# First attention of a gated cross-attention kernel on one Trainium2 core: 154 keys split as 128 and 26 in place of 77 and 77

## The chip, the core and the metric

The kernel is one program on one NeuronCore of a Trainium2 chip. The metric is device time in microseconds (us), the median of several executions. The engines are TensorE (PE in the rows, its weight loads PEld), VectorE (DVE), ScalarE (ACT), GpSimd (POOL) and SyncE (SP). PSUM has eight banks of 128 partitions by 512 fp32 values.

## The reference

Two blocks in series, each a gated cross-attention and a gated feed-forward part, with a residual stream x of 2 x 1024 tokens of 256 values. The change is in the first of the four parts:

```
x = x + tanh(g_xattn[0]) * xattn0(layernorm(x), ctx, ctx, W, b)     # the part that changes
x = x + tanh(g_ffn[0])   * ffn0(layernorm(x), Wg, Wu, Wd)            # 8 experts, all of them for every token
x = x + tanh(g_xattn[1]) * xattn1(layernorm(x), ctx, mask, ...)      # 8 heads of 64
x = x + tanh(g_ffn[1])   * ffn1(layernorm(x), wg, We, be)            # one of 8 experts by argmax, with a capacity

def xattn0(query, key, value, W, b):        # one head of 256; ctx is 2 x 154 x 256
    q, k, v = query @ W.T + b, key @ W.T + b, value @ W.T + b
    return softmax(q @ k.T / 16) @ v
```

## The kernel before

All engines run programs written out by hand, tied by semaphores: an engine takes its own instructions in the order written, and the order below is the whole schedule. Nothing is planned or reordered by a tool.

The 2048 tokens are 16 tiles of 128, and 4 chunks (`u` = 0 to 3) of 4 tiles; chunks 0 and 1 belong to batch 0, 2 and 3 to batch 1. In the first attention keys and values are the same tensor k0 = ctx @ W.T + b, held transposed as `k0T` (feature on the partition, 308 keys along the row). TensorE's preparation ends with `v_transposes` (L1307 to L1316): eight transposes of 128 x 77 pieces of `k0T` into banks 1 and 2, which ScalarE copies to `V0` (L970), keys on 77 partitions, two halves for each batch.

For each chunk TensorE then does, in the loop after L1379:

- `a_scores` (L1333): scores of four tiles, two per bank, in banks 4 and 5 or 6 and 7 (`UNIT_PS`). From chunk 2 on each of its two halves waits for `a_res`, the residual add of that half two chunks earlier (L1338).
- `a_p_transposes` (L1349): eight transposes of the exponentials `PA`, 77 keys of a tile at a time, into banks 1 and 2. ScalarE copies them to `PTA` (L936).
- the transposes of a later chunk's normed rows (L1296), `x1_transposes` or `x2_transposes`.
- `a_attend` (L1356): for each tile two matmuls over 77 keys each, `PTA` against `V0`, added up in half a bank. After tiles 0 and 1 it signals the first half on `a_out_ps`, after tiles 2 and 3 the second (L1362).

An fp32 matmul is two records in the trace, an fp32 transpose one. VectorE takes row maxima (`a_maxes`, L1947, L1952), and adds the attention into `x_res` (`a_add`, L1968), two tiles for each half, with a signal on `a_res` after each half. Its list in order after chunk 0's maxima is: norm of chunk 2, maxima 1, statistics 3, `a_add(0)`, maxima 2, statistics of chunk 0's result, small mask work, `a_add(1)`, statistics, maxima 3, norm, `a_add(2)`, then sums and roundings of the operands of the first feed-forward part (`xop_raw` L1978, `xop_lo` L490), `a_add(3)` among them. GpSimd splits expert weights between its small steps (L619 to L661); each round starts at a norm of VectorE (`pool.wait_ge(a_ln1, 2)`, then `a_ln2, 1`).

Bank 5 (`R0_PS`) holds the bias row's product until VectorE has read it (L1929, L1931), and after that chunk 0's scores of tiles 2 and 3.

## Time and profile before

| | us |
|---|---|
| median of 3 executions | 1226.97 (1226.01 to 1227.29) |
| span of the profiled execution | 1225.2 |
| that execution's own time | not listed apart from the span; the median is 1.8 above the span |
| TensorE busy | 1199.5 (98% of the span) |
| VectorE busy | 1051.4 (86%) |
| ScalarE busy | 739.6 (60%) |
| GpSimd busy | 886.6 (72%) |
| first attention, in the span | about 18 to 54 |
| first feed-forward part | 54 to about 998 |

The span runs from the first to the last instruction of the profiled execution. A busy share says nothing by itself: the feed-forward part is nine tenths of the span, and the change lies ahead of it, in a stretch where several engines wait for one another.

### The profile page before, as it was taken

The numbers are of one execution on the slowest core, as the hardware profiler recorded it, in microseconds if no ns is written. First come the engines' busy times: TensorE is split into PE (matmuls) and PEld (weight loads), VectorE is DVE, ScalarE is ACT, GpSimd is POOL, SyncE is SP. The second block draws the span as 40 slices with busy tenths as digits, with TensorE's granted clock in tenths as the row PEclk, the third lists the DMA queues.
The fourth block names the chain that finished last, engine by engine and source line by source line (L and its number), as shares of the span: only waits on it lengthen the run. The fifth ranks groups of instructions, "written<-read, shape, count | busy, mean of one in ns | idle before, by whom it ended". The sixth has DMA issues, their size and how long they took to land.

```text
span 1225.2 us, 18428 instructions
## 1 busy us (share of the span) xinstructions
PE 1199.5 (98%) x6143; PEld 987.8 (81%) x6143; DVE 1051.4 (86%) x1754; ACT 739.6 (60%) x1531; POOL 886.6 (72%) x848
## 2 busy tenths in 40 slices
...
DMA packets 42365, 48.27 MB, mean 39 GB/s; under 512 B 4239, under 2 KB 40143, under 8 KB 42015
## 3 DMA queue, kind: packets, MB, share of 16 engines
...
## 4 chain that ended last, share of the span: by engine, by line
PE 89%; DVE 5%; ACT 3%; issue 1%; ACTq 1%; POOL 0%; POOLq 0%; DVEq 0%
PE bank L1400 25%; PE bank L1402 25%; PE bank L1401 25%; ACT PC L1124 3%; PE bank L1643 2%; PE bank L1652 1%; PE bank L1822 1%; DVE nmC L2204 1%; PE bank L1805 1%; PE bank L1345 1%; PE bank L1755 1%; DVE stats L1879 1%; PE bank L1577 1%; PE bank L1627 1%; PE bank L1578 1%
## 5 line engine op out<-in xcount | busy, mean ns | idle before, releaser
L1400 PE MATMUL bank<-xop_hi,w_hi 128*128 128x512 f32 x896 | 349.2, 390 | 1.9 <-DVE half_g L2028 0.9
L1402 PE MATMUL bank<-xop_hi,w_lo 128*128 128x512 f32 x896 | 348.6, 389 | 0.0
L1401 PE MATMUL bank<-xop_lo,w_hi 128*128 128x512 f32 x896 | 348.6, 389 | 0.0
L2063 DVE TENSOR_TENSOR hid_lo<-hid,hid_hi 128x512 fp32r<-128x512 f32 x228 | 232.5, 1044 | 6.0 <-ACT hid_hi L1042 6.0
L1400 PEld LDWEIGHTS bank<-xop_hi,w_hi 128*128 128x128 f32 x896 | 168.2, 188 | 37.9 <-DVE half_g L2028 1.3
L1402 PEld LDWEIGHTS bank<-xop_hi,w_lo 128*128 128x128 f32 x896 | 168.2, 188 | 35.0
L1401 PEld LDWEIGHTS bank<-xop_lo,w_hi 128*128 128x128 f32 x896 | 168.2, 188 | 34.7
L1042 ACT CAST hid_hi<-hid 128x512 fp32r<-128x512 f32 x228 | 140.8, 622 | 63.6 <-PE bank L1402 38.3
L1026 ACT ACTIVATE s<-bank 128x512 f32<-128x512 f32 x128 | 78.2, 611 | 95.2 <-PE bank L1402 95.2
L1400 PE MATMUL bank<-hid_hi,wd_hi 128*128 128x512 f32 x344 | 134.2, 390 | 0.7 <-DVE hid_lo L2063 0.6
L1401 PE MATMUL bank<-hid_lo,wd_hi 128*128 128x512 f32 x344 | 133.9, 389 | 0.0
L1402 PE MATMUL bank<-hid_hi,wd_lo 128*128 128x512 f32 x344 | 133.9, 389 | 0.0
L1002 ACT COPY bank<-bank 128x512 f32<-128x512 f32 x128 | 73.2, 573 | 67.9 <-PE bank L1402 67.9
L2087 DVE TENSOR_TENSOR acc<-bank,acc 128x512 f32<-128x512 f32 x136 | 93.0, 684 | 20.4 <-PE bank L1402 20.3
L1032 ACT ACTIVATE half_g<-half_g 128x512 f32<-128x512 f32 x128 | 81.1, 634 | 46.8 <-DVE half_g L2036 25.5
L2055 DVE TENSOR_TENSOR hid<-half_u,half_g 128x512 f32<-128x512 f32 x128 | 107.2, 875 | 0.0
L702 POOL TENSOR_TENSOR t_loT<-t_rawT,t_hiT 128x512 fp32r<-128x512 f32 x56 | 84.2, 1526 | 16.4 <-ACT t_hiT L1049 16.4
L2046 DVE TENSOR_TENSOR hid<-bank,s 128x512 f32<-128x512 f32 x128 | 86.6, 676 | 1.2 <-PE bank L1402 1.2
L648 POOL TENSOR_TENSOR w_lo<-w_raw,w_hi 128x1024 fp32r<-128x1024 f32 x32 | 77.5, 2421 | 2.9 <-ACT w_hi L1063 2.9
L796 POOL TENSOR_TENSOR PC<-PC,rdenC 128x616 f32<-128x616 f32 x32 | 38.9, 1216 | 53.5 <-DVE rdenC L2212 53.4
L1400 PEld LDWEIGHTS bank<-hid_hi,wd_hi 128*128 128x128 f32 x344 | 64.6, 188 | 15.3 <-DVE hid_lo L2063 1.0
L1402 PEld LDWEIGHTS bank<-hid_hi,wd_lo 128*128 128x128 f32 x344 | 64.6, 188 | 13.5
(288 smaller groups left out, 2608.3 us busy)
## 6 DMA issues: line engine op xcount, KB each, us to landing
...
```

Of the source, the lines that this page charges most:

```text
L648: nc.gpsimd.tensor_tensor(out=lo[:, :, W_S1:W_S4 + 1], in0=s[:, :, W_S1:W_S4 + 1], in1=hi[:, :, W_S1:W_S4 + 1].bitcast(F32), op=ALU.subtra ...
L702: nc.gpsimd.tensor_tensor(out=t_lo[i][:], in0=t_raw[i][:], in1=t_hi[i][:].bitcast(F32), op=ALU.subtract).then_inc(t_ready, 1)
L1026: nc.scalar.activation(out[:], ps[:], ACT.Silu).then_inc(silu_ready[h], 1)
L1032: nc.scalar.activation(half["g"][:], half["g"][:], ACT.Silu).then_inc(silu_ready[h], 1)
L1042: nc.scalar.copy(hid_hi[n % 2][h][:], hid[h][:]).then_inc(hi_ready[h], 1)
L1400: mm(ps, w, a, start=start, stop=False, skip_group_check=True)
L1401: mm(ps, w, a_low, start=False, stop=False, skip_group_check=True)
L1402: return mm(ps, w_low, a, start=False, stop=True, skip_group_check=True)
L2046: nc.vector.tensor_tensor(out=hid[h][:], in0=ps[:], in1=s[:], op=ALU.mult).then_inc(hid_ready[h], 1)
L2055: nc.vector.tensor_tensor(out=hid[h][:], in0=half["u"][:], in1=half["g"][:], op=ALU.mult).then_inc(hid_ready[h], 1)
L2063: nc.vector.tensor_tensor(out=hid_lo[n % 2][h][:], in0=hid[h][:], in1=hid_hi[n % 2][h][:].bitcast(F32), op=ALU.subtract).then_inc(lo_ready ...
L2087: nc.vector.tensor_tensor(out=to, in0=ps, in1=to, op=ALU.add).then_inc(acc_added, 1)
```

## The change

The 154 keys of a batch are taken as 128 and 26. The two tiles of an output bank pair use different ends: tiles 0 and 1 of a chunk (`i` = 0) take keys 0 to 127 and then 128 to 153, tiles 2 and 3 (`i` = 1) take keys 26 to 153 and then 0 to 25. The rests stand on partitions 0 to 25 for `i` = 0 and 32 to 57 for `i` = 1, so that the matmuls over 26 keys of two tiles in different banks use different row groups of TensorE. `PA` gets slots of 160 columns, the last six of them set to zero once by GpSimd, so that the rests of two tiles can be transposed together as 64 columns. `V0` holds, for each batch, both choices of 128 keys, and a new `V0R` the rests; eight matmuls by the identity, 26 keys each, make them in bank 5. ScalarE's wait and signal counts move by one, and TensorE's wait for the values (`V0_OUT`) now stands ahead of the second half of chunk 0's scores, since that half uses bank 5.

```diff
     B, S, D = x.shape
     KEYS = ctx.shape[1]
     KH = KEYS // 2
+    REST, RW = KEYS - P, 32
+    SLOT = P + RW
+    FIRST_KEY, REST_KEY = (0, REST), (P, 0)
+    V0R_PS = 5
     NE0, _, F = Wg.shape
     INNER = Wq.shape[1]
     HD = 64
...
     C_VALUES = 2 + HB // 2
     PREP_DVE = 4
-    NORMED0, A0_OUT, V0_OUT, NORMED20 = 5, 6, 8, 9
+    NORMED0, A0_OUT, V0_OUT, NORMED20 = 5, 6, 9, 10
     R_MID, R_LOW = 32, 64
     R_ROWS = R_LOW + 1
-    PREP_PE = 10
+    PREP_PE = 11
     FIRST_SEVEN = 3
...
-        V0 = keep.take("V0", [KH, 2 * B, D], F32)
+        V0 = keep.take("V0", [P, B, 2, D], F32)
+        V0R = keep.take("V0R", [2 * RW, B, D], F32)
         stats, mv, ve, rstd, shift = [], [], [], [], []
...
-        PA = sa.take("PA", [P, 2 * CT, KEYS], F32)
-        PTA = sa.take("PTA", [KH, 2, 2, CH], F32)
+        PA = sa.take("PA", [P, 2 * CT * SLOT], F32)
+        PTA = sa.take("PTA", [P, 2, CH], F32)
+        PTR = sa.take("PTR", [2 * RW, 2, 2 * P], F32)
         nmA, nmsA, denA, rdenA, coefA = (sa.take(n, [P, NT], F32) for n in ("nmA", "nmsA", "denA", "rdenA", "coefA"))
         mask8 = sa.take("mask8", [P, AK], U8, size=1)
...
+            steps.did(nc.gpsimd.memset(PA[:].rearrange("p (n k) -> p n k", k=SLOT)[:, :, KEYS:SLOT], 0.0))
...
                     n = u * CT + j
-                    ins = nc.scalar.activation(PA[:, u % 2 * CT + j, :], bank[UNIT_PS[u % 2][j // 2]][:, j % 2 * 256:j % 2 * 256 + KEYS], ACT.Exp,
+                    at = (u % 2 * CT + j % 2 * 2 + j // 2) * SLOT
+                    ins = nc.scalar.activation(PA[:, at:at + KEYS], bank[UNIT_PS[u % 2][j // 2]][:, j % 2 * 256:j % 2 * 256 + KEYS], ACT.Exp,
                                                bias=nmsA[:, n:n + 1], scale=D ** -0.5, accum_out=denA[:, n:n + 1])
                 ins.then_inc(a_probs, 1)
 
             def a_pT_out(u):
-                for k in range(2):
-                    act.wait_ge(a_pT_ps, 2 * u + k + 1)
-                    nc.scalar.copy(PTA[:, u % 2, k, :], bank[PT_PS[k]][0:KH, :]).then_inc(a_pT, 1)
+                act.wait_ge(a_pT_ps, 2 * u + 1)
+                nc.scalar.copy(PTA[:, u % 2, :], bank[PT_PS[0]][:]).then_inc(a_pT, 1)
+                act.wait_ge(a_pT_ps, 2 * u + 2)
+                nc.scalar.copy(PTR[:, u % 2, :], bank[PT_PS[1]][0:2 * RW, 0:2 * P]).then_inc(a_pT, 1)
 
             def x_raw_out(u):
...
             a_xnT_out(0)
+            for b in range(B):
+                act.wait_ge(prep_pe, 9 + b)
+                nc.scalar.copy(V0[:, b, :, :].rearrange("p k d -> p (k d)"), bank[V0_PS[b]][:]).then_inc(prep_act, 1)
+            act.wait_ge(prep_pe, 11)
             for i in range(2):
-                act.wait_ge(prep_pe, 9 + i)
-                nc.scalar.copy(V0[:, 2 * i:2 * i + 2, :].rearrange("p k d -> p (k d)"), bank[V0_PS[i]][0:KH, :]).then_inc(prep_act, 1)
+                row = slice(i * RW, i * RW + REST)
+                ins = nc.scalar.copy(V0R[row, :, :].rearrange("p b d -> p (b d)"), bank[V0R_PS][row, :])
+            ins.then_inc(prep_act, 1)
             a_xnT_out(1)
...
                 pe.wait_ge(prep_dve, 4)
+                for b in range(B):
+                    for i in range(2):
+                        key = b * KEYS + FIRST_KEY[i]
+                        for m in range(KB):
+                            ins = tr(bank[V0_PS[b]][:, i * D + m * P:i * D + (m + 1) * P], k0T[:, m, key:key + P], ident[:])
+                    ins.then_inc(prep_pe, 1)
                 for i in range(2):
-                    for r in range(2):
+                    for b in range(B):
+                        key = b * KEYS + REST_KEY[i]
                         for m in range(KB):
-                            ins = tr(bank[V0_PS[i]][0:KH, r * D + m * P:r * D + (m + 1) * P],
-                                     k0T[:, m, (2 * i + r) * KH:(2 * i + r + 1) * KH], ident[:])
-                    ins.then_inc(prep_pe, 1)
+                            ins = mm(bank[V0R_PS][i * RW:i * RW + REST, b * D + m * P:b * D + (m + 1) * P],
+                                     k0T[:, m, key:key + REST], ident[:], start=True, stop=True, skip_group_check=True)
+                ins.then_inc(prep_pe, 1)
 
...
                 pe.wait_ge(a_probs, u + 1)
-                for k in range(2):
-                    for j in range(CT):
-                        ins = tr(bank[PT_PS[k]][0:KH, j * P:(j + 1) * P], PA[:, u % 2 * CT + j, k * KH:(k + 1) * KH], ident[:])
-                    ins.then_inc(a_pT_ps, 1)
+                first = u % 2 * CT * SLOT
+                for j in range(CT):
+                    i, a = j // 2, j % 2
+                    at = first + (2 * a + i) * SLOT + FIRST_KEY[i]
+                    ins = tr(bank[PT_PS[0]][:, j * P:(j + 1) * P], PA[:, at:at + P], ident[:])
+                ins.then_inc(a_pT_ps, 1)
+                for a in range(2):
+                    at = first + 2 * a * SLOT + P
+                    ins = tr(bank[PT_PS[1]][0:2 * RW, a * P:(a + 1) * P], PA[:, at:at + 2 * RW], ident[:])
+                ins.then_inc(a_pT_ps, 1)
 
             def a_attend(u):
                 pe.wait_ge(a_pT, 2 * u + 2)
-                for j in range(CT):
-                    for k in range(2):
-                        ins = mm(bank[UNIT_PS[u % 2][j // 2]][:, j % 2 * D:(j % 2 + 1) * D], PTA[:, u % 2, k, j * P:(j + 1) * P],
-                                 V0[:, u // CB * 2 + k, :], start=k == 0, stop=k == 1)
-                    if j % 2:
-                        ins.then_inc(a_out_ps, 1)
+                b = u // CB
+
+                def out_of(i, a):
+                    return bank[UNIT_PS[u % 2][i]][:, a * D:(a + 1) * D]
+
+                for a in range(2):
+                    for i in range(2):
+                        j = 2 * i + a
+                        mm(out_of(i, a), PTA[:, u % 2, j * P:(j + 1) * P], V0[:, b, i, :], start=True, stop=False)
+                    for i in range(2):
+                        row = slice(i * RW, i * RW + REST)
+                        ins = mm(out_of(i, a), PTR[row, u % 2, a * P:(a + 1) * P], V0R[row, b, :], start=False, stop=True)
+                        if a == 1:
+                            ins.then_inc(a_out_ps, 1)
 
             def x2_transposes(u):
                 pe.wait_ge(a_xnT, KB * NC)
...
             pe.wait_ge(prep_dve, 4)
             a_scores(0, [0])
             x1_transposes(1)
+            pe.wait_ge(prep_act, V0_OUT)
             a_scores(0, [1])
             for u in range(NC):
                 if u + 1 < NC:
                     a_scores(u + 1)
-                if u == 0:
-                    pe.wait_ge(prep_act, V0_OUT)
                 a_p_transposes(u)
                 if u + 2 < NC:
                     x1_transposes(u + 2)

```

On TensorE, in the preparation and chunk 0, the rows were these (`k0T` keys transposed, `ones_r` the bias part of the scores, `A` their weights, `xnA` normed rows):

```order
L1314 MATMUL bank<-ident,k0T 77x128 [waits prep_dve,prep_act]
L1314 MATMUL bank<-ident,k0T 77x128 x7
L1340 MATMUL bank<-r_56,ones_r 128x2x154 [waits a_xnT,prep_dve]
L1345 MATMUL bank<-A_55,xnT 128x154 x4
L1296 MATMUL bank<-ident,xnA 128x128 [waits a_ln1,a_xnT]
L1296 MATMUL bank<-ident,xnA 128x128 x7
L1340 MATMUL bank<-r_56,ones_r 128x2x154 [waits a_xnT]
```

Now they are:

```order
L1329 MATMUL bank<-ident,k0T 128x128 [waits prep_dve,prep_act]
L1329 MATMUL bank<-ident,k0T 128x128 x7
L1335 MATMUL bank<-ident,k0T 26x128 x8
L1361 MATMUL bank<-r_56,ones_r 128x2x154 [waits a_xnT,prep_dve]
L1366 MATMUL bank<-A_55,xnT 128x154 x4
L1310 MATMUL bank<-ident,xnA 128x128 [waits a_ln1,a_xnT]
L1310 MATMUL bank<-ident,xnA 128x128 x7
L1361 MATMUL bank<-r_56,ones_r 128x2x154 [waits a_xnT,prep_act]
```

Eight small matmuls came in ahead of the first scores, and the second half of the scores waits for ScalarE as well. Also on TensorE, the transposes of the exponentials and the values' matmuls of one chunk, before:

```order
L1353 MATMUL bank<-ident,PA 77x128 [waits a_probs]
L1353 MATMUL bank<-ident,PA 77x128 x7
L1296 MATMUL bank<-ident,xnA 128x128 [waits a_ln1,a_xnT]
L1296 MATMUL bank<-ident,xnA 128x128 x7
L1360 MATMUL bank<-V_57,PTA 128x256 [waits a_pT]
L1360 MATMUL bank<-V_57,PTA 128x256 x7
```

and now:

```order
L1376 MATMUL bank<-ident,PA 128x128 [waits a_probs]
L1376 MATMUL bank<-ident,PA 128x128 x3
L1380 MATMUL bank<-ident,PA 64x128 x2
L1310 MATMUL bank<-ident,xnA 128x128 [waits a_ln1,a_xnT]
L1310 MATMUL bank<-ident,xnA 128x128 x7
L1393 MATMUL bank<-V_57,PTA 128x256 [waits a_pT]
L1393 MATMUL bank<-V_57,PTA 128x256
L1396 MATMUL bank<-V0R,PTR 128x256 x2
L1393 MATMUL bank<-V_57,PTA 128x256 x2
L1396 MATMUL bank<-V0R,PTR 128x256 x2
```

Eight transposes became six; eight matmuls over 77 keys became four over 128 and four over 26, with tiles 0 and 2 ahead of tiles 1 and 3. On ScalarE the copies of the values, before and now:

```order
L923 COPY xnT<-bank 128x512 [waits a_xnT_ps] x2
L970 COPY V_57<-bank 77x512 [waits prep_pe] x2
L923 COPY xnT<-bank 128x512 [waits a_xnT_ps] x2
```

```order
L930 COPY xnT<-bank 128x512 [waits a_xnT_ps] x2
L979 COPY V_57<-bank 128x512 [waits prep_pe] x2
L983 COPY V0R<-bank 26x512 [waits prep_pe]
L983 COPY V0R<-bank 26x512
L930 COPY xnT<-bank 128x512 [waits a_xnT_ps] x2
```

Two copies of the rests came in between.

## Rows read from the trace of the kernel before

**Rows 1.** The page: busy time of TensorE, share of the span, instructions.
```profile
PE 1199.5 (98%) x6143; PEld 987.8 (81%) x6143; DVE 1051.4 (86%) x1754; ACT 739.6 (60%) x1531; POOL 886.6 (72%) x848
```
**Rows 2.** Busy time in two stretches, with the granted clock (of 1) after PEclk.
```profile
40.62:49.88 9.26, 9.26 (x65) 8.69 (x66) 7.45 (x25) 6.09 (x18) 5.75 (x10) 1.00 0.27 87
66.39:1225.20 1158.81, 1140.75 (x5823) 941.41 (x5823) 1001.00 (x1608) 699.92 (x1436) 850.71 (x772) 1.00 0.11 37
```
**Rows 3.** Timeline of TensorE, preparation's end: start, us, engine, line, operation, count, [idle before].
```profile
19.01 1.07 PE L1314 MATMUL bank<-ident,k0T 128*77 128x128 f32 x8 [0.34 <-DVE A L1938]
...
21.10 1.04 PE L1296 MATMUL bank<-ident,xnA 128*128 128x128 f32 x8
...
22.11 1.21 PE L1345 MATMUL bank<-A,xnT 128*128 128x154 f32 x8
```
**Rows 4.** Timeline of ScalarE, the same stretch.
```profile
19.68 1.07 ACT L970 COPY V<-bank 77x512 f32<-77x512 f32 x2 [0.33 <-PE bank L1314]
```
**Rows 5.** Timeline of TensorE, chunks 0 and 2, values and what follows.
```profile
27.60 3.72 PE L1360 MATMUL bank<-V,PTA 77*128 77x256 f32 x16
31.39 0.29 PE L1340 MATMUL bank<-r,ones_r 65*128 65x308 bf16 x1
...
40.62 0.29 PE L1340 MATMUL bank<-r,ones_r 65*128 65x308 bf16 x1 [1.39 <-DVE x_res L1968]
...
44.74 3.72 PE L1360 MATMUL bank<-V,PTA 77*128 77x256 f32 x16
```
**Rows 6.** Timeline of TensorE, second attention: 64 rows on two groups, then 128.
```profile
1059.77 0.70 PE L1604 MATMUL bank<-k1T,qT 64*128 64x154 f32 x8
1060.40 0.33 PE L1511 MATMUL bank<-ident,acc 128*128 128x128 f32 x1
```
**Rows 7.** Timeline of TensorE, second attention: 128 columns of output, then 64.
```profile
1066.59 0.55 PE L1627 MATMUL bank<-ident,PC 128*128 128x128 f32 x3
1067.08 2.24 PE L1643 MATMUL bank<-PTC,V 128*64 128x128 f32 x34
```
**Rows 8.** Timeline of VectorE, chunk 0's add to chunk 2's maxima.
```profile
33.95 0.48 DVE L1947 TENSOR_REDUCE nmA<-bank 128x2 f32<-128x308 f32 x1 [0.70 <-PE bank L1345]
34.47 1.60 DVE L1952 TENSOR_SCALAR nmsA<-nmA 128x4 f32<-128x4 f32 x1
...
39.60 1.66 DVE L1968 SCALAR_TENSOR_TENSOR x_res<-bank,coefA,x_res 128x256 f32<-128x256 f32 x4
```
**Rows 9.** Timeline of VectorE, chunk 2's add and after it.
```profile
44.11 0.17 DVE L1952 TENSOR_SCALAR nmsA<-nmA 128x4 f32<-128x4 f32 x1
...
48.56 0.88 DVE L1968 SCALAR_TENSOR_TENSOR x_res<-bank,coefA,x_res 128x256 f32<-128x256 f32 x2 [0.85 <-PE bank L1360]
49.88 0.69 DVE L1978 TENSOR_TENSOR xop_raw<-bank,xop_raw 128x512 f32<-128x512 f32 x1 [0.44 <-PE bank L1296]
50.60 0.82 DVE L490 TENSOR_TENSOR xop_lo<-xop_raw,xop_hi 128x512 fp32r<-128x512 f32 x1
```
**Rows 10.** Timeline of GpSimd, three of its steps.
```profile
25.41 0.72 POOL L619 TENSOR_TENSOR w_raw<-raw_gu 128x256 f32<-128x256 f32 x1 [2.10 <-DVE xnA L1892]
...
33.68 2.37 POOL L648 TENSOR_TENSOR w_lo<-w_raw,w_hi 128x1024 fp32r<-128x1024 f32 x1
...
49.84 1.04 POOL L632 CAST w_hi<-w_raw 128x1024 fp32r<-128x1024 f32 x1
```
**Rows 11.** The chain that ended last, where TensorE's unbroken stretch begins.
```profile
66.39 0.50 PE bank L1400
```
**Rows 12.** Lengths of one record or weight load, ns: least/median/most, first and last start.
```profile
L1604 PE MATMUL bank<-k1T,qT x256: 288/291/291, 1020.0 to 1163.8; 64*128 64x154 f32 x128
...
L1643 PE MATMUL bank<-PTC,V x544: 270/273/472, 1028.2 to 1178.5; 128*64 128x128 f32 x171, 80*64 80x128 f32 x11
...
L1360 PEld LDWEIGHTS bank<-V,PTA x64: 186/190/190, 27.6 to 53.2; 77*128 77x128 f32 x64
L1360 PE MATMUL bank<-V,PTA x64: 379/379/483, 27.6 to 53.4; 77*128 77x256 f32 x64
```

## The prediction

> **What bounds the kernel now.** I read the busy shares first: TensorE is busy for 98% of the span [rows 1]. That alone would say that less work on TensorE is less time, so I read by stage. From 66.39 to the end TensorE works for 1140.75 of 1158.81 us [rows 2], and the chain of waits that ended last passes to TensorE at 66.39 [rows 11]. All that the change touches lies before. So the question is by how much the moment at 66.39 moves; what is behind it moves along.
>
> Ahead of it the chain alternates. From 19.01 TensorE carries it through the transposes of the keys and the first scores [rows 3]. From chunk 2's maxima (33.95) to the end of chunk 1's adds VectorE does [rows 8], and TensorE waits 1.39 us for it until 40.62 [rows 5]. From 40.62 to 49.88 TensorE is busy for 9.26 of 9.26 us [rows 2] at the full granted clock (1.00, its 2.4 GHz level), and VectorE waits for it twice (0.85 and 0.44 us) [rows 9]. Then VectorE carries it again.
>
> There is a second thing to see in VectorE's rows. A setting of four numbers per partition (L1952) takes 0.17 us at 44.11 [rows 9] but 1.60 at 34.47, ending at 36.07 [rows 8]; GpSimd's L648 ran from 33.68 to 36.05 [rows 10]. At 50.60 an L490 takes 0.82 and ends at 51.42 [rows 9]; GpSimd's L632 ends at 50.88 [rows 10]. I read both as VectorE being held until GpSimd's instruction ends. GpSimd's round starts when VectorE's norm is done (25.41) [rows 10], so it moves with the chain at its start.
>
> **The change, part by part.**
>
> *Values, in the preparation.* Eight transposes stay eight, at the same pace: eight of 77 columns take 1.07, eight of 128 take 1.04 [rows 3]. A record costs (1.04 - 0.27)/7 = 0.11, 0.27 being the last one's own length [rows 12]. Added are eight matmuls of 26 keys, 16 records of 128 columns, for which the trace has no row. The nearest is L1643, whose outputs also alternate between two column groups: 34 records in 2.24 us, (2.24 - 0.27)/33 = 0.06 each [rows 7], so two run side by side. Here one column group has the first four matmuls, the other the last four. Side by side they cost 8 x 0.11 = 0.88, one after the other 16 x 0.11 = 1.76.
>
> *Changes of tile shape.* From 64 rows back to 128, the last pair starts at 59.77 + 0.70 - 0.29 = 60.18 and the next instruction at 60.40: 0.22, where the pace is (0.70 - 0.29)/3 = 0.13 [rows 6, 12]. From 128 columns to 64, the last starts at 66.59 + 0.55 - 0.27 = 66.87 and the next at 67.08: 0.21 for 0.11 [rows 7]. So a change costs 0.09 to 0.10; I take 0.09. The values pay two: 0.88 + 0.18 = **+1.06**, all of it on the path, since the scores stand behind them in TensorE's list. The other end is 1.76 + 0.18 = 1.94. I take the lower, because L1643 ran side by side although each of its matmuls is two records as well.
>
> The Trainium skill (TensorE: Matmul & The Clock Gate, section Part 3: Packing small matmuls) says against this that matmuls keep strict program order, with no reordering. By that rule the second column group would start only with the end of the first, and this term would be near 1.8.
>
> *The new wait and the copies.* ScalarE copies two rests more, 1.07 for two copies of 512 columns [rows 4]. They can start near 19.01 + 0.88 + 1.06 + 0.2 = 21.2 and end at 22.3. TensorE reaches the wait at 21.10 + 0.88 + 1.06 = 23.04 [rows 3]: nothing, with 0.7 to spare. ScalarE's next copy, queued behind, waits for transposes that are later by 1.06 as well. Were the rests serial, copies and wait would both be later by the same. GpSimd's added memset of 48 columns is covered by the warm-up matmuls. Nothing.
>
> *Transposes of the exponentials.* Eight become six, with two changes if 64 columns are a shape of their own: 6 x 0.11 + 0.18 = 0.84 against 0.88, -0.04 for each chunk; -0.22 without the changes, +0.18 if 64 columns need two records each. ScalarE copies 64 x 256 in place of 77 x 512 and isn't later.
>
> *The values' matmuls.* A record of 256 columns costs (3.72 - 0.38)/15 = 0.22 [rows 5, 12]; sixteen were 3.56. Now four full matmuls are 8 records, the two pairs of rests 4 paces if they run side by side as L1604's two row groups do (eight records in 0.70) [rows 6], and four changes 0.36: 12 x 0.22 + 0.36 = 3.03. That is -0.53 for each chunk. With nothing side by side it is +0.36.
>
> *The late half.* The first half used to be signalled after half of the records. Now tiles 0 and 1 are done only when nearly all is. I follow it chunk by chunk.
>
> Chunk 0. Its values start at 27.60 + 1.06 - 0.04 = 28.62 and end 3.72 - 0.62 = 3.10 later, at 31.72 (one change comes after the end). VectorE starts 0.1 later (48.56 behind 44.74 + 3.72), adds a half in 0.88 [rows 5, 9], and TensorE follows 0.13 after: chunk 2's scores start at 32.83 in place of 31.39 [rows 5], +1.44. VectorE's L1952 could then end near 34.47 + 1.44 + 0.17 = 36.1. But GpSimd holds it to 36.05 + 1.06 = 37.11 anyway. Behind L1952 the shift is +1.06 again: the late half has cost nothing, with 1.0 to spare.
>
> Chunk 1. Its values end near 40.0, VectorE wants them at 39.60 + 1.06 = 40.66 [rows 8]. Nothing, gain included.
>
> Chunk 2. Start 44.74 + 1.06 - 0.04 = 45.76, end 48.86, adds from 48.96, and four of them take 1.58 to the next instruction (1.66 less the overlap) [rows 8]: the first operand sum starts at 50.54 in place of 49.88, +0.66. Here 0.4 of the gain would show. But the L490 behind it meets GpSimd's L632, which now ends at 50.88 + 1.06 = 51.94, later than the 51.26 at which L490 starts. It ends 0.54 behind it as before [rows 9, 10]: +1.06.
>
> Chunk 3's values end about when they did, and the feed-forward part behind them waits for VectorE. Nothing.
>
> **The sum** is +1.06 at 66.39, a span of 1225.2 + 1.1 = 1226.3. What lies around the span (1.8 to the median of the runs) is taken as unchanged: 1226.97 + 1.1 = **1228.0**.
>
> **The rivals.** About 0.2% (2.5 us) is what a measurement of this kernel can tell from no change.
>
> *Not held.* If VectorE's long instructions aren't tied to GpSimd's end, chunk 0's L1952 ends at 36.1 and the shift falls to about 0. Chunk 2's values then end near 47.8, VectorE's adds near 49.5: -0.3, **1226.6**. Against it stand two ends that agree to 0.02 us [rows 8, 10]; for it, that phases of two engines are hard to foresee. 0.15.
>
> *In order.* If tiles are served in program order, the rests in the preparation overlap in one record only (+1.83) and each pair of rests takes three paces (+0.44 for each chunk). Chunk 0 is still covered by the hold; the end is +1.83, **1228.8**. Against it stands L1604 [rows 6]; for it, that four matmuls in a row on one group are more than any row shows. 0.22.
>
> *Dear changes, slower.* TensorE changes shape six times in each chunk and twice before. The 0.09 is from shapes of 64. If with 26 rows the array finishes a record (0.38) and then loads weights (0.19) with nothing overlapped [rows 12], a change costs 0.57 - 0.22 = 0.35. Then the preparation costs 1.58, each chunk's transposes +0.48 and its values about +0.51. Chunk 0's scores are late by over 3.4, past the cover of the hold, and the shift behind L1952 becomes about 2.1; chunk 2 brings it to +2.9, **1229.9**, slower. It decides from about 0.3 for each change. 0.13. The Trainium skill (TensorEngine Tiling (Array Packing), section Key Properties) says that changing the tiling mode drains the TensorE, and gives no figure; by it every one of these changes pays, and this rival is a matter of how much.
>
> Something that no row shows, either way: 0.08.
>
> **How the numbers follow.** My forecast has 0.42, in order 0.22, not held 0.15, dear changes 0.13, the unknown 0.08. The range of 8 in 10 reaches from not held less the scatter of the runs (1226.6 - 0.8) to a little over dear changes: 1225.8 to 1230.2. Slower by over 0.2% are dear changes and half of the unknown, 0.17; faster has no mechanism that I can price, 0.05 for the unknown and a lucky phase; within 0.2% 0.78. The predicted time is 1228.0.
>
> **What would show it.** In the profile after: eight matmuls L1335 in about 1.1 us (1.9 if in order); no wait ahead of the second scores; 16 records of `a_attend` in 3.1 in place of 3.72 (3.5 in order, 4.1 with nothing side by side); chunk 2's scores about 1.4 later, with L1952 ending when L648 does; TensorE's unbroken stretch from about 67.45. I am wrong if the feed-forward part changes its pace, if a change of shape takes over 0.2, or if L1952 is short while the shift behind it stays.

## The result, and the profile after

The changed kernel takes 1230.24 us, the median of five runs (1227.36 to 1232.03), against 1226.97 for five of the kernel before (1224.33 to 1227.33); the ratio is 1.0029, with a 95% interval of 1.0018 to 1.0040. I had forecast 1228.0 and a range up to 1230.2. So the change is slower by over 0.2%, the case to which I had given 0.17. Two further comparisons of the same kernel gave 1.0018 (1.0009 to 1.0027) and 1.0027 (1.0018 to 1.0036), with medians of 1229.62 and 1229.98. So 1230.24 lies just above the range, the two repeats just inside it; all three are well above 1228.0.

The profiled execution is the fastest of the five: 1227.36 us, with a span of 1225.6. Its span is within 0.4 us of that of the profile of before, although the medians are 3.3 apart. That is the first thing to explain. First the page of the changed kernel (answers to [rows 1]) and its stretches (to [rows 2]); the page rows give busy time, share of the span and instructions.

```profile
PE 1197.9 (98%) x6151; PEld 982.2 (80%) x6151; DVE 1049.6 (86%) x1754; ACT 739.8 (60%) x1533; POOL 886.2 (72%) x849
```
```profile
40.32:49.34 9.02, 9.02 (x63) 7.39 (x64) 7.28 (x24) 5.76 (x18) 5.56 (x9) 1.00 0.27 89
66.07:1225.60 1159.53, 1140.82 (x5823) 941.10 (x5823) 999.70 (x1608) 699.63 (x1436) 850.35 (x772) 1.00 0.11 37
```

The preparation and chunk 0's values on TensorE (timeline: start, us, engine, line, operation, count, [idle before]); these answer to [rows 3, 5].

```profile
15.90 1.04 PE L1310 MATMUL bank<-ident,xnA 128*128 128x128 f32 x8
17.17 1.06 PE L1329 MATMUL bank<-ident,k0T 128*128 128x128 f32 x8 [0.24 <-DVE A L1972]
18.17 1.52 PE L1335 MATMUL bank<-ident,k0T 128*26 128x128 f32 x16
19.61 0.30 PE L1361 MATMUL bank<-r,ones_r 65*128 65x308 bf16 x1
...
25.43 0.66 PE L1376 MATMUL bank<-ident,PA 128*128 128x128 f32 x4
25.92 0.38 PE L1380 MATMUL bank<-ident,PA 128*64 128x128 f32 x2
26.14 1.04 PE L1310 MATMUL bank<-ident,xnA 128*128 128x128 f32 x8
27.02 1.13 PE L1393 MATMUL bank<-V,PTA 128*128 128x256 f32 x4
28.08 0.70 PE L1396 MATMUL bank<-V0R,PTR 26*128 26x256 f32 x4
28.71 1.13 PE L1393 MATMUL bank<-V,PTA 128*128 128x256 f32 x4
29.77 0.70 PE L1396 MATMUL bank<-V0R,PTR 26*128 26x256 f32 x4
31.60 0.29 PE L1361 MATMUL bank<-r,ones_r 65*128 65x308 bf16 x1 [1.12 <-DVE x_res L2002]
...
66.07 0.50 PE L1434 MATMUL bank<-xop_hi,w_hi 128*128 128x512 f32 x1 [0.23 <-DVE half_u L2062]
```

The eight rest matmuls (L1335) take 1.52 us, neither the 1.1 of the forecast nor the 1.9 of the rival in order. Chunk 0's values take 29.77 + 0.70 - 27.02 = 3.45 in place of 3.72; I had written 3.1. Next, the holds on VectorE (to [rows 8 to 10]): VectorE, then GpSimd.

```profile
34.67 1.09 DVE L1986 TENSOR_SCALAR nmsA<-nmA 128x4 f32<-128x4 f32 x1
...
50.06 1.06 DVE L496 TENSOR_TENSOR xop_lo<-xop_raw,xop_hi 128x512 fp32r<-128x512 f32 x1
```
```profile
33.37 2.37 POOL L655 TENSOR_TENSOR w_lo<-w_raw,w_hi 128x1024 fp32r<-128x1024 f32 x1
...
49.54 1.04 POOL L639 CAST w_hi<-w_raw 128x1024 fp32r<-128x1024 f32 x1
```

L1986 ends at 35.76, GpSimd's L655 at 35.74. L496 ends at 51.12, 0.54 behind the end of GpSimd's L639 at 50.58, as it did before. Both holds are there as forecast. The other traces bear the first one out: in 19 of the 20 traces of this case the setting for chunk 2 takes 0.6 to 1.6 us and ends 0.02 to 0.03 behind GpSimd's instruction. In the twentieth (e1) GpSimd is done first, and the same setting takes 0.17. VectorE and GpSimd in e1:

```profile
38.23 0.17 DVE L1986 TENSOR_SCALAR nmsA<-nmA 128x4 f32<-128x4 f32 x1
```
```profile
35.27 2.35 POOL L655 TENSOR_TENSOR w_lo<-w_raw,w_hi 128x1024 fp32r<-128x1024 f32 x1
```

Not every instruction of GpSimd holds it, though: chunk 3's setting takes 0.17 (43.81 to 43.98) while GpSimd's L602, a power of 4 elements per partition, runs from 43.09 to 44.10. The Trainium skill (SBUF — State Buffer, section SBUF: two separate sides) says that GpSimd and those instructions of VectorE that are in a two-port mode or have two inputs in SBUF share a pair of ports, held for the whole instruction by whichever starts first. The ends beside L655 and L639 agree; no run here shows the ports, and L602 is a case in which nothing waited.

**One clock for all traces.** The start of the attention differs from execution to execution, since before it, between about 9 and 16 us, TensorE's granted clock is at 0.50 for 0, 3.4 or 6.8 us. So I measure from the start of chunk 0's row transposes (L1310, before L1296) to five starts on TensorE behind it. The last is the feed-forward matmul that waits for `half_u`, where TensorE's unbroken stretch begins (66.39 before [rows 11], 66.07 after). Each number is a difference of two starts in the timeline of TensorE; "low" is where the granted clock reads 0.50 between 16 us and that point.

| kernel | first scores | chunk 0 values | chunk 2 scores | chunk 3 scores | unbroken stretch | low at |
|---|---|---|---|---|---|---|
| before, as shown | 2.28 | 9.96 | 13.75 | 22.98 | 48.75 | none |
| before again (e15) | 1.85 | 9.54 | 13.32 | 22.55 | 48.32 | none |
| before again (e18) | 2.11 | 9.78 | 13.57 | 22.78 | 50.20 | 41.3 |
| after, as shown | 3.71 | 11.12 | 15.70 | 24.42 | 50.17 | none |
| change again (e1) | 3.69 | 11.09 | 15.66 | 25.80 | 51.55 | 33.8 |
| change again (e12) | 3.39 | 10.79 | 15.36 | 24.09 | 51.15 | 42.8 |
| change again (e16) | 3.39 | 10.80 | 15.37 | 24.10 | 49.87 | none |
| change again (e17) | 3.39 | 10.80 | 15.37 | 24.11 | 51.18 | 43.1 |

The rows behind the first and the last column for e15, then for e16: start of the row transposes, first scores, unbroken stretch.

```profile
18.92 1.04 PE L1296 MATMUL bank<-ident,xnA 128*128 128x128 f32 x8
20.77 0.29 PE L1340 MATMUL bank<-r,ones_r 65*128 65x308 bf16 x1
...
67.24 0.50 PE L1400 MATMUL bank<-xop_hi,w_hi 128*128 128x512 f32 x1 [0.24 <-DVE half_u L2028]
```
```profile
19.22 1.04 PE L1310 MATMUL bank<-ident,xnA 128*128 128x128 f32 x8
22.61 0.30 PE L1361 MATMUL bank<-r,ones_r 65*128 65x308 bf16 x1
...
69.09 0.50 PE L1434 MATMUL bank<-xop_hi,w_hi 128*128 128x512 f32 x1 [0.23 <-DVE half_u L2062]
```

The two traces first shown each have a small wait ahead of the key transposes (0.34 and 0.24) that e15, e12, e16 and e17 don't have. Without a low stretch the change moves the unbroken stretch by 49.87 - 48.32 = +1.55 (or 50.17 - 48.75 = +1.42). With one it comes 1.3 to 1.4 later still, and 1.6 in the kernel before (e18, measured from its first scores). Behind it the change costs nothing by itself: in the nine traces of this case without a low stretch in the second attention, of both kinds of kernel, the rest of the span is 1157.8 to 1158.2. In the eleven with one, starting between 1070 and 1119 us, it is 1158.8 (before, as shown) to 1159.8 (e12). So there is a second place where the clock falls, at a price of 0.8 to 1.8. Four of the five traces of the change have it (all but e17), one of the three of the kernel before. Over all kernels tried it is 8 of 15 with the split of 128 and 26, and 3 of 5 with 77 and 77, so nothing says that the change brings it.

The profile after looks good because its clock was full from the start (chunk 0's row transposes begin at 15.90, before at 17.64), and because it has no low stretch in the first attention: -1.74 to the row transposes, +1.42 to the unbroken stretch and +0.7 behind it make the 0.4. For the same reason the unbroken stretch begins at 66.07 and not at the 67.45 of the forecast, although the chain ahead of it is longer.

### The profile page after: what moved, and what is told of

Its sections match the earlier page's. It is cut to its first block, busy times and chain, and to the rows that moved or that the text cites. A ratio compares the mean times of both kernels' runs of the same rounds, so it can differ in the third digit from the quotient of the medians.

```text
span 1225.6 us, 18447 instructions
## 1 busy us (share of the span) xinstructions
PE 1197.9 (98%) x6151; PEld 982.2 (80%) x6151; DVE 1049.6 (86%) x1754; ACT 739.8 (60%) x1533; POOL 886.2 (72%) x849
## 4 chain that ended last, share of the span: by engine, by line
PE 89%; DVE 5%; ACT 4%; issue 1%; ACTq 1%; POOL 0%; POOLq 0%; DVEq 0%
PE bank L1434 25%; PE bank L1435 25%; PE bank L1436 25%; ACT PC L1138 3%; PE bank L1686 2%; PE bank L1677 1%; PE bank L1856 1%; DVE nmC L2238 1%; PE bank L1839 1%; DVE stats L1913 1%; PE bank L1366 1%; PE bank L1789 1%; PE bank L1611 1%; PE bank L1612 1%; PE bank L1616 1%
## 5 line engine op out<-in xcount | busy, mean ns | idle before, releaser
L655 POOL TENSOR_TENSOR w_lo<-w_raw,w_hi 128x1024 fp32r<-128x1024 f32 x32 | 77.4, 2420 | 2.9 <-ACT w_hi L1077 2.9
```

The costliest lines, as they stand in the source:

```text
L655: nc.gpsimd.tensor_tensor(out=lo[:, :, W_S1:W_S4 + 1], in0=s[:, :, W_S1:W_S4 + 1], in1=hi[:, :, W_S1:W_S4 + 1].bitcast(F32), op=ALU.subtra ...
```

## The experiments

Two theories are named in them. CLOCK: part of the loss is a granted clock that falls in the first attention. DIRECT: all of it is the work and waits of the change. PREPARATION, CHUNKS, SHAPE and PLACE are explained where they come. A *fall* is a low stretch that begins in the first attention behind a wait of TensorE.

**e1, the change again.**

> The changed kernel as it is, once more, for the clock and the span of each execution. In the five executions so far the mean granted clock was 0.998 in the one at 1227.36 and 0.994 to 0.996 in those at 1230.1 to 1232.0. Theory CLOCK: most of the 3.3 us is TensorE at its lower level in more stretches than before; then time falls with the granted clock along one line (about 1.2 us for each 0.001), an execution at 0.998 is near 1227.4, and a trace at 0.996 or less has stretches of granted clock 0.5 that the kernel before doesn't have, between 8 and 60 us or in the second attention. Theory DIRECT: instructions on the path (the values' rests at 1.5 us, the late half) make it; then the before and changed kernels differ by 3 us at the same granted clock, and the trace of an execution at 1230 shows the first feed-forward part starting 3 us later with no stretch at 0.5 between.

1229.62 us (1227.49 to 1231.37), ratio 1.0018. Its trace has the low stretch at 33.8 (table); this is what the stretches before and in it look like (columns as in [rows 2]).

```profile
30.30:33.80 3.50, 2.38 (x15) 1.31 (x12) 2.93 (x7) 1.37 (x7) 3.36 (x6) 0.99 0.01 2
33.80:37.10 3.30, 3.30 (x15) 3.19 (x15) 0.81 (x2) 1.71 (x4) 3.30 (x3) 0.50 0.00 0
```

TensorE was busy for 2.38 of 3.50 us, with its wait of 1.12 in them, and then ran chunk 2's scores at the 1.2 GHz level. My forecast had a granted clock of 1.00 for this stage from one trace, and asked no further. CLOCK was expected here to be most of the 3.3 us. That has not held: at an equal granted clock 1.9 us are left (under e16 to e18).

**e2, filled once.** Five wide matmuls of ones into a free bank behind chunk 0's values.

```diff
                 a_attend(u)
+                if u == 0:
+                    keep_busy(5, PT_PS[0])
```

> The change, with five warm-up matmuls (bf16, 128 x 512, 0.22 each, 1.1 in all) behind chunk 0's values, into bank 1, where TensorE waits 1.12 us for the late half. Theory CLOCK, if this wait is what lets the clock fall: the executions lose their low stretches, median near 1227.5 (-2.7). If the clock falls elsewhere: no change, 1230.2. Theory DIRECT: 1230.2 to 1230.5, since the fill lies in a wait.

1228.55 us, ratio 1.0015 (1.0006 to 1.0024); no low stretch in the attention; 50.06 to the unbroken stretch. That is 1.1 us under e1 in the median, but the intervals overlap, and CLOCK had expected 1227.5. By itself it settles nothing.

**e3, the first half early.** Tile by tile, its rest right behind its first matmul.

```diff
-                for a in range(2):
-                    for i in range(2):
+                for i in range(2):
+                    for a in range(2):
...
+                    ins.then_inc(a_out_ps, 1)
```

> The change, with the values' matmuls tile by tile (128 keys, then 26), tiles 0 and 1 first, so that the first half is signalled after half of the work again, and no two rests stand side by side. Each chunk's values take 16 records and 8 changes of shape, 16 x 0.22 + 8 x 0.08 = 4.2 in place of 3.0. Theory DIRECT (late half costs): chunk 2's scores start right behind the values (0.1) and the kernel is at or below the change (1229 to 1230). If the pairing is worth what it takes off TensorE: slower by up to 1.2 for chunk 2, 1231.4. Theory CLOCK: TensorE is busier between 26 and 40, so fewer low stretches: 1228 to 1229.

1230.65 us (1229.23 to 1231.86), ratio 1.0025 (1.0014 to 1.0035), and 51.56 to the unbroken stretch with no low clock: 1.7 later than e16. The chunks had been expected to become dearer, but CLOCK, which had 1228 to 1229 here, missed. The rows of its values:

```profile
29.93 0.70 PE L1393 MATMUL bank<-V,PTA 128*128 128x256 f32 x2
30.55 0.69 PE L1395 MATMUL bank<-V0R,PTR 26*128 26x256 f32 x2
31.18 0.70 PE L1393 MATMUL bank<-V,PTA 128*128 128x256 f32 x2
31.81 0.69 PE L1395 MATMUL bank<-V0R,PTR 26*128 26x256 f32 x2
```

Two records take 0.63 from start to start where the pace is 2 x 0.215 = 0.43 (0.22 in [rows 5, 12]). So each change of shape costs 0.20. In the profile after, 28.71 - 27.02 = 1.69 holds six paces (1.29) and two changes: 0.20 each again. I had 0.09. I had looked only at the interval across the change (0.31 here, 0.22 and 0.21 in [rows 6, 7]); the record behind it is late too (0.32). Splitting the pairs up to have the first half early is a loss.

**e4, alternating column groups.** The rest matmuls of the preparation in another order.

```diff
-                for i in range(2):
-                    for b in range(B):
-                        for m in range(KB):
+                for b in range(B):
+                    for m in range(KB):
+                        for i in range(2):
```

> The change, with the eight matmuls of the rests in the preparation in alternating order of their two column groups. They took 1.52 us in the group's order (0.08 for each record). If side by side works best when neighbours differ: 16 records in 1.1 to 1.2 us, and everything behind earlier by 0.35. If the order doesn't matter (the array looks ahead): 1.5 again. Time: -0.35 or 0 against the change at the same granted clock; theory CLOCK expects the scatter of 1227 to 1232 to stay.

1228.60 us (1226.62 to 1229.74), ratio 1.0013 (1.0004 to 1.0022). The same sixteen records:

```profile
20.20 1.06 PE L1335 MATMUL bank<-ident,k0T 128*26 128x128 f32 x16
21.19 0.30 PE L1361 MATMUL bank<-r,ones_r 65*128 65x308 bf16 x1
```

1.06 in place of 1.52. Matmuls on two column groups run fully side by side when they alternate in the list. When four of one group stand ahead of four of the other, only part of it overlaps. The starts of single records in the profile after tell how much: the first group's eight go from 18.17 to 18.95, 0.11 apart, and the second group's first starts at 18.63 beside the fifth of them. Four records of eight overlap, so there are 12 paces and not 16 or 8. (Which record is whose is my reading of the spacing; the trace does not name the groups.) The first scores start 0.46 earlier (2.93), and so does all behind (49.35 in e7, which has this order and no low stretch).

**e5, the values alone.** The rests of the preparation are replaced by two wide matmuls of ones; the remainders' values are left out.

```diff
-                for i in range(2):
-                    for b in range(B):
...
+                    ins = mm(bank[V0R_PS][i * RW:i * RW + REST, :], ones_r[:, 0:REST],
+                             ones_r[:].unsqueeze(1).to_broadcast([P, 4, P]), start=True, stop=True, skip_group_check=True)
```

> The change with the preparation's eight matmuls of remainders (fp32, 128x26) replaced by two wide bf16 matmuls of ones into the same bank, so that V0R holds a constant: the remainders' values are left out, all else stands. It splits the change into preparation and chunks. Theory PREPARATION (what the change costs at an equal granted clock, 1.9 us against the kernel before, is the matmuls of remainders, 1.52 us in their group, and the copies behind them): the median falls to 1226.0 to 1227.2, ratio 0.9992 to 1.0003, and chunk 0 begins some 1.0 us earlier than in the change. Theory CHUNKS (the shorter values are given back, and more, in chunks 1 and 2 by the late half, whatever the preparation does): the median stays above 1228.0, and the waits of the scores for x_res grow by what the preparation gave. If the clock falls in the first attention because of the chunks' own rhythm, this kernel may still show granted clocks of 0.996 or 0.995 in as many executions as the change did (6 of 11).

1227.50 us (1225.80 to 1233.20), ratio 1.0008 (0.9995 to 1.0020); the median is 0.3 above the kernel before's in its batch (1227.19). That lies between PREPARATION, the theory that the preparation makes the loss at an equal clock (1226.0 to 1227.2), and CHUNKS, the theory that the chunks make it whatever the preparation does (over 1228.0). The traces decide, below.

**e6, the preparation alone.** The kernel before with the eight rest matmuls, their copies and the wait.

```diff
+                for i in range(2):
+                    for b in range(B):
+                        key = b * KEYS + REST_KEY[i]
+                        for m in range(KB):
+                            ins = mm(bank[V0R_PS][i * RW:i * RW + REST, b * D + m * P:b * D + (m + 1) * P],
+                                     k0T[:, m, key:key + REST], ident[:], start=True, stop=True, skip_group_check=True)
+                ins.then_inc(prep_pe, 1)
```

> The kernel before with the change's added preparation alone: eight fp32 matmuls of remainders into bank 5 behind its own transposes, their two copies on ScalarE (into space that is free by then, read by nobody), and the wait for them ahead of the second half of chunk 0's scores. Attention stays 77 and 77. Theory PREPARATION: ratio 1.0010 to 1.0016 (1.2 to 1.9 us above before: 1.5 us of matmuls, a shift of all that follows), and the group of remainders reads 1.4 to 1.6 us. Theory CHUNKS: at most 0.6 us (ratio under 1.0005), since the waits of the scores for DVE (1.39 us at chunk 3) take the shift up. On the clock: if it falls because of the change's narrower instructions in the chunks, this kernel's granted clocks read like the kernel before's (mean 0.9967); if any later start of the chunks is enough, they read lower (0.9963).

1228.60 us, 1.4 above 1227.19; ratio 1.0010 (1.0000 to 1.0021). Where a kernel has its first scores tells where it ends:

| kernel | first scores | chunk 2 scores | chunk 3 scores | unbroken stretch | low at |
|---|---|---|---|---|---|
| before again (e15) | 1.85 | 13.32 | 22.55 | 48.32 | none |
| values alone (e5) | 2.26 | 14.24 | 22.98 | 48.74 | none |
| preparation alone (e6) | 3.39 | 14.86 | 24.09 | 51.43 | 42.7 |
| alternating (e4) | 2.93 | 14.91 | 23.64 | 50.68 | 41.9 |
| alternating, filled (e7) | 2.93 | 14.90 | 23.62 | 49.35 | none |
| change, filled (e13) | 3.38 | 15.37 | 24.10 | 49.87 | none |

From the first scores on, e5 is 0.41 behind e15 and 0.42 at the end; e7 1.08 and 1.03; e13 1.53 and 1.55. What the chunks lose (chunk 2's scores are late by 0.5 more, in e5, e7 and e13) is gone at chunk 3's scores, and what they gain is gone too. So in traces without a fall the preparation's shift is the whole loss: PREPARATION stands, CHUNKS has fallen.

**e7, alternating and filled; e8, the kernel before filled.** Wide matmuls of ones in TensorE's waits: four behind chunk 0's values and five behind chunk 1's; in e8 the five alone.

```diff
                 a_attend(u)
+                if u < 2:
+                    keep_busy(4 + u, PT_PS[0])
```

> The alternating order of the preparation's remainders (1.06 us in place of 1.52 us) together with wide bf16 matmuls of ones in two waits of TensorE in the first attention: four behind chunk 0's values and five behind chunk 1's. Theory CLOCK (part of what is lost comes from a lower granted clock in the first attention, which falls in or behind these waits): no stretch at 0.50 between 30 and 50 us of the profile, mean granted clock over the runs at least as high as the kernel before's in the same batch, and the median at 1226.8 to 1227.6, ratio 0.9997 to 1.0006. Theory DIRECT (the clock's stretches come whatever TensorE does there, and the fillers only lengthen the queue): median 1228.6 or more, as the alternating order alone gave (ratio 1.0013), and clocks as there (mean 0.9965).

> The kernel before with five wide bf16 matmuls of ones behind chunk 1's values, where its TensorE waits 1.39 us for x_res. Theory CLOCK: the kernel before has low stretches in the first attention in some of its executions as well; then this one is faster by up to 0.8 us in the median (ratio 0.9993 to 1.0000) and its mean granted clock is above 0.9967. Theory DIRECT, and also if the kernel before never falls there: no change (0.9998 to 1.0004), the same clocks as before, and its only cost a start of chunk 3's scores later by under 0.1 us.

e7: 1228.22 us, ratio 1.0005 (0.9996 to 1.0014), mean granted clock 0.9970, no low stretch in the attention. The median lies between CLOCK's (up to 1227.6) and DIRECT's (1228.6 or more). e4 had 1.0013: the sign is CLOCK's, the size within the intervals. e8: 1.0002 (0.9994 to 1.0011), mean granted clock 0.9966; this is what DIRECT expected. Filling does not help the kernel before by anything that can be measured.

**e9 to e11, two other ways of building it; e12, the change once more.** e9 puts a chunk's four first matmuls ahead of its four rests: two changes of shape, not four. For this a second accumulation group is started in a bank while the first is open, and the values come out different, so e9 and e11 tell of time alone. e10 gives both tiles of a pair keys 0 to 127 as their firsts, so that `V0` needs four transposes and the rests four matmuls. e11 is both.

```diff
-                    for i in range(2):
+                for a in range(2):
+                    for i in range(2):
                         row = slice(i * RW, i * RW + REST)
```
```diff
-    FIRST_KEY, REST_KEY = (0, REST), (P, 0)
+    FIRST_KEY = (0, 0)
...
+                        ins = mm(bank[V0R_PS][0:REST, b * D + m * P:b * D + (m + 1) * P],
+                                 k0T[:, m, key:key + REST], ident[:], start=True, stop=True, skip_group_check=True)
...
+                ins = nc.scalar.copy(V0R[i * RW:i * RW + REST, :, :].rearrange("p b d -> p (b d)"), bank[V0R_PS][0:REST, :])
```

> The change with each chunk's values in the order four tiles' firsts, then four rests, so two changes between 128-row and 26-row matmuls in a chunk in place of four. In the profile of the change a matmul behind such a change starts 0.31 us and the one after it 0.32 us behind its predecessor, against 0.214 us within a kind: 0.20 us a change, where I had taken 0.09. Theory SHAPE (that price is real, and belongs to the change of rows): a chunk's values read 3.0 to 3.1 us in place of 3.45. The end gains less, as the waits for x_res in chunks 2 and 3 take part of it: 0 to 0.8 us below the change, ratio 1.0012 to 1.0022 where the change has 1.0018 in the same kind of batch. Rival PLACE (the price comes from changing the bank or the accumulation group, not the rows): the values stay above 3.3 us.

> Another way to build the same split: both tiles of a pair take keys 0 to 127 first and keys 128 to 153 as rest. Then V0 needs four transposes in place of eight and one copy, the remainders four matmuls in place of eight, copied twice to rows 0 and 32; the price is that the rests of the probabilities need four small matmuls a chunk in place of two 64-column ones. Theory PREPARATION (1.5 of the 1.9 us that the change costs at an equal granted clock are its preparation): the preparation's matmuls take about 0.9 us less than the change's and no more than the kernel before's; median 1226.3 to 1227.6, ratio 0.9993 to 1.0004. If CHUNKS were right the time would stay at 1.0015 or more. Known extra cost: 0.1 to 0.3 us a chunk for the two added matmuls.

> Both edits at once, the shared first keys and the grouped order of the values: the version that would keep the change's gain (12 passes for 16) and drop its two prices. If both theories hold (PREPARATION and SHAPE): 1225.4 to 1227.0, ratio 0.9987 to 1.0000. If the waits of scores for x_res are what sets the pace of the first attention, whatever TensorE saves, it is equal to the kernel with the shared keys alone, within 0.3 us.

> The change as it is, in this batch, as the base for the three others and for the clock: over the first 11 and 5 executions its mean granted clock was 0.9961, the kernel before's 0.9968 over 65. Theory CLOCK (the change brings more low stretches, one in two executions): mean again 0.9958 to 0.9964 and below the kernel before's in the same batch, median 1229.2 to 1230.2, ratio 1.0015 to 1.0030. Rival CHANCE (those clocks were luck): the mean equals the kernel before's within 0.0003, and the ratio is 1.0012 to 1.0018, what an equal clock gives.

The values of e9:

```profile
29.78 1.99 PE L1393 MATMUL bank<-V,PTA 128*128 128x256 f32 x8
31.71 1.13 PE L1398 MATMUL bank<-V0R,PTR 26*128 26x256 f32 x8
```

31.71 + 1.13 - 29.78 = 3.06, as SHAPE said: two changes fewer save 0.39, although the banks alternate as before. So a change between 128 and 26 rows costs 0.20, and PLACE, which put it on the bank or the accumulation group, has fallen. Only the 0.09 across it is sure to be the rows': the first value record of every chunk is followed by the next at 0.32 as well, also in the kernel before, where no such change stands. The end did not move by what can be measured: ratio 1.0021 (1.0010 to 1.0032). e10's preparation is shorter as expected (first scores at 2.49), yet it took 1229.75, ratio 1.0016 (1.0006 to 1.0025), with a low stretch at 42.7 in its trace; my expectation of 1226.3 to 1227.6 was missed. e11 took 1227.74, ratio 1.0007 (0.9998 to 1.0017), above its 1225.4 to 1227.0 as well. None of the three is faster than the kernel before. e12, in the same batch, took 1229.98, ratio 1.0027, with a mean granted clock of 0.9956. Here are its stretches around the second wait, and the rows of the wait.

```profile
39.00:42.80 3.80, 2.42 (x14) 1.34 (x15) 3.52 (x16) 2.32 (x11) 2.53 (x5) 1.00 0.00 0
42.80:46.20 3.40, 3.40 (x15) 3.29 (x15) 2.82 (x12) 0.97 (x2) 1.53 (x2) 0.51 0.42 137
46.20:50.00 3.80, 3.80 (x28) 3.00 (x26) 2.74 (x8) 2.69 (x8) 1.34 (x4) 0.99 0.26 89
```
```profile
42.65 0.29 PE L1361 MATMUL bank<-r,ones_r 65*128 65x308 bf16 x1 [1.38 <-DVE x_res L2002]
42.78 2.19 PE L1366 MATMUL bank<-A,xnT 128*128 128x154 f32 x8
44.76 0.46 PE L1361 MATMUL bank<-r,ones_r 65*128 65x308 bf16 x1
```

Eight records of scores take 2.19 us, which elsewhere take 1.21.

**e13 and e14, both waits filled; e15, the kernel before again.** e13 is the change with e7's fillers, e14 is e10 with them.

> The change with wide bf16 matmuls of ones in both waits of TensorE in the first attention, four behind chunk 0's values and five behind chunk 1's; nothing else moved. Base: the change repeated, ratio 1.0027, mean granted clock 0.9956, a stretch at 0.50 at 42.8 us in its profile. Theory CLOCK (about 1 of its 3 us is a clock that falls behind the second wait): no stretch at 0.50 between 30 and 50 us, mean clock 0.9968 to 0.9972, ratio 1.0009 to 1.0017, so 1 us or more under the plain change. Rival DIRECT (filling changes nothing that costs, the runs with fillers had fewer low stretches by luck): ratio 1.0020 or more and mean clock under 0.9965.

> The shared first keys (preparation 0.9 us shorter than the change's) together with the same fillers in both waits. The shared version alone gave 1.0016 with a stretch at 0.50 at 42.8 us and a mean clock of 0.9965. Theories CLOCK and PREPARATION together: no low stretch between 30 and 50 us, mean clock 0.9968 or more, ratio 0.9998 to 1.0008; below 0.9998 it would be the better version. Rival DIRECT: 1.0014 or more.

> The kernel before once more, under its own name, for its trace: of it there is only one, with no stretch at 0.50 between 16 and 1108 us. Theory CLOCK says that the kernel before is mostly spared in the first attention: no low stretch between 30 and 50 us, mean clock 0.9965 to 0.9971, ratio 0.9997 to 1.0003. Rival (any kernel here falls behind its wait of 1.39 us, and the trace shown was luck): a low stretch at 40 to 46 us here too, and then the change's lower mean clock has another place.

e13: 1228.94 us (1227.14 to 1230.14), ratio 1.0014 (1.0005 to 1.0023), mean granted clock 0.9967. The same stretches and rows as in e12:

```profile
39.00:42.80 3.80, 3.60 (x19) 1.74 (x19) 3.52 (x16) 2.32 (x11) 2.44 (x5) 1.00 0.00 0
42.80:46.20 3.40, 3.40 (x29) 3.37 (x30) 3.30 (x13) 1.52 (x4) 1.54 (x2) 1.00 0.29 88
```
```profile
41.29 1.25 PE L1284 MATMUL bank<-ones_r 128*128 128x512 bf16 x5
42.74 0.29 PE L1361 MATMUL bank<-r,ones_r 65*128 65x308 bf16 x1 [0.20 <-DVE x_res L2004]
42.87 1.21 PE L1366 MATMUL bank<-A,xnT 128*128 128x154 f32 x8
```

TensorE's wait is 0.20 in place of 1.38, the clock stays at 1.00, the scores take 1.21, and the unbroken stretch comes 51.15 - 49.87 = 1.28 earlier than in e12. The Trainium skill (TensorE: Matmul & The Clock Gate, section Part 1: The HAM clock gate) says that activity of TensorE releases its throttle and lack of it brings it back. The pair e12 and e13 agrees, but it is no proof of what the fillers do: e16 is the same kernel as e12, waits the same 1.38 us unfilled, and stays at 1.00. e14 took 1228.34, ratio 1.0010 (1.0001 to 1.0019): lower than the change's ratios, not better than before, and above the 0.9998 to 1.0008 that I had expected. Its two added matmuls a chunk give back what its preparation saves: chunk 0's transposes of the exponentials take 27.93 - 26.79 = 1.14 where e13's take 28.55 - 27.84 = 0.71, from chunk 3's scores to the feed-forward part, two chunks, it needs 13.28 where e13 needs 12.84, and the unbroken stretch comes at 49.97 (e13 49.87). e15: ratio 1.0000 (0.9991 to 1.0009), no low stretch in the attention.

**e16 to e18, three more traces: two of the change, one of the kernel before.**

> One look at the change, for a further trace of it: of three, one has no stretch at 0.50 in the first attention, one has it at 33.8 us and one at 42.8 us. Theory CLOCK: this one has it with a chance of 2 in 3, between 30 and 46 us, and then the last wait of the feed-forward part's start ends 51.0 to 51.6 us behind the start of chunk 0's transposes; without it 49.9 to 50.2 us. Rival DIRECT: none, and still over 51 us.

> A second look at the change, the same question: a stretch at 0.50 between 30 and 46 us with a chance of 2 in 3, and 51.0 to 51.6 us with it, 49.9 to 50.2 us without it. If neither look has one, I have overrated how often it comes and more of the change's loss is without a place.

> One more look at the kernel before: neither of its two traces has a stretch at 0.50 between 16 and 1100 us. Theory CLOCK: none here either, and 48.3 to 48.8 us from the start of chunk 0's transposes to the last wait of the feed-forward part's start. A low stretch at 40 to 46 us would say that the kernel before pays it too, now and then.

e16 has none and e17 has one at 43.1 (table in the first section). e18 corrected me: the kernel before has it too, at 41.3, behind its own wait of 1.38:

```profile
37.80:41.30 3.50, 2.12 (x11) 1.59 (x11) 3.25 (x15) 1.76 (x6) 2.78 (x5) 0.99 0.00 0
41.30:44.70 3.40, 3.40 (x16) 3.30 (x15) 2.57 (x11) 0.71 (x2) 1.53 (x3) 0.51 0.48 163
```

So the fall is no new kind of event. Three of five traces of the change have it, one of three of the kernel before, and none of the five kernels with fillers (e2, e7, e8, e13, e14). Of the other kernels e4, e6, e9 and e10 have it, e3, e5 and e11 don't. Only e1's lies behind chunk 0's values, the wait that the change adds. All others lie behind the second wait, which the kernel before has too: 7 of the 15 traces in which that wait is unfilled, none of the 4 in which it is filled (e7, e8, e13, e14). Traces are too few to say how often; the granted clock of every execution is known, though (± is the standard error):

| kernel | executions | mean granted clock | mean us |
|---|---|---|---|
| before (four batches and e15) | 136 | 0.9968 ± 0.0001 | 1227.05 |
| change (first five, e1, e12) | 27 | 0.9959 ± 0.0003 | 1229.92 |
| change, both waits filled (e13) | 11 | 0.9967 ± 0.0003 | 1228.83 |

Within the change's executions 0.001 of clock goes with 0.9 us, so its lower clock is 0.0009 x 0.9 / 0.001 = 0.8 us. That number is of the whole span and doesn't say where the clock was low. The traces don't place it either: averaged over its five, the change is 2.7 us longer than the average of the three before, 1.7 of it up to the unbroken stretch and 1.1 behind it, where the second attention's low stretches are. At a clock of 0.998 or more the change has a mean of 1227.7 (four executions) and the kernel before 1225.8.

The best evidence on the place comes from three pairs that differ in the fillers alone: e13 and the change, e7 and e4, e14 and e10. Against the kernel before in the same batch:

| | executions | mean granted clock | mean us above before |
|---|---|---|---|
| split, unfilled (e1, e12, e4, e10) | 44 | 0.9962 ± 0.0002 | 2.3 ± 0.2 |
| split, both waits filled (e13, e7, e14) | 34 | 0.9970 ± 0.0002 | 1.3 ± 0.2 |
| 77 and 77, its wait filled (e8) | 12 | 0.9966 ± 0.0003 | 0.1 ± 0.2 |

All three pairs go the same way, by 0.9, 0.4 and 1.1 us. The two of a pair ran in different batches.

## Why the prediction was wrong

Two steps failed: the size of the term +1.06, and the clock, which the sum had at nothing. The clock is the larger of the two.

**The rests in the preparation: "+1.06, all of it on the path".** It is on the path, and it is 1.53 (3.38 against 1.85 to the first scores). That alone is e6's loss. The two changes of shape in it were priced about right (0.20 in place of 0.11 from start to start on the way into the rests, the same on the way out, by the starts of single records). What was wrong is 0.88 for 8 paces: there are 12, which is 1.31. I had seen two side by side in L1643 [rows 7], whose matmuls alternate, and took it for four in a row. I had named that doubt ("more than any row shows") and gave it to the rival in order. The rule that I cited against myself, of strict program order, would have had 1.8: measured are 1.52 in this order and 1.06 when alternating, so neither reading was right; the order in the list decides. Nor did the matmuls start in strict program order, as the starts given under e4 show. With 1.53 in place of 1.06 the forecast would have been 1228.5, still 1.7 short.

**The changes of shape, "I take 0.09": 0.20.** The bound of "over 0.2" was just met. (One reading was rounded wrongly: (0.70 - 0.29)/3 is 0.14, so that change is 0.08.) A chunk's values take 3.45 and not 3.1. For the end it cost nothing, since the chunks' gains and losses are both hidden.

**Transposes of the exponentials.** 26.14 - 25.43 = 0.71 in the profile after, 0.66 in chunks 1 and 2; forecast 0.84, before 0.87 to 0.91. Smaller than either, since the two changes to and from 64 columns cost nothing here (records start 0.11 apart across them), and hidden as well.

**The copies and the new wait: nothing.** Right. The second scores have no wait.

**The late half, held.** Right in mechanism. Chunk 2's scores came 15.37 - 13.32 = 2.05 later, of which 0.5 beyond the preparation (forecast 0.4). GpSimd's hold covered it: chunk 3's scores are late by 1.55, the start's own shift. The second hold (L496, L639) did the same for chunk 2's gain in the change's two traces without a fall. Behind a fall at the second wait it is absent (L496 takes 0.69), since GpSimd is done by then. Not held, in order and dear changes have all fallen: there are holds, the rests partly overlap, and 0.20 is under the 0.3 from which dear changes decide. 1229.9 was close to the measured time for a reason that isn't there.

**What I didn't ask: the granted clock.** I read 1.00 for one stretch of one execution [rows 2] and costed the chunks with it. TensorE waits over 1 us for `x_res` once in the kernel before and twice in the changed one (1.12 and 1.37), because the late half turned the first passage into a wait. Behind such a wait the clock can read 0.50, which costs 1.3 to 1.6 us. This step is missing from the sum. By the mean granted clock the loss of clock is worth about 0.8, over the whole span; by the three pairs filling the two waits gives back about 1.0. I had also let everything behind 66.39 move along unchanged; a low stretch there, in either kernel, adds 0.8 to 1.8.

**The sum now.** 1.55 from the traces (e16 against e15, no fall in either) plus 0.8 from the clock is 2.3. The measured difference is 2.9 in the means, and 3.6, 2.2 and 3.3 by the ratios of the three comparisons.

**Open.** About 0.5 us has no place: at a granted clock of 0.998 or more the two kernels still differ by 1.9, where the traces give 1.55. That the clock falls more often in the change is shown by the mean over 27 executions; which part of the change does it is not: the preparation alone has a mean of 0.9968 and the values alone 0.9964, 12 executions each, too few to part them. That the falls in the first attention are where the change loses clock is likely, not shown. For it stands what fillers give back in the three pairs and don't in the kernel before. Against it stands that five of the six falls in split kernels lie behind a wait that the kernel before has as well, and that none in 4 against 7 in 15 can be chance. The gain in the change's own ratio (1.0027 to 1.0014) has intervals that overlap a little.
